# A two-layer decoder on one core: the second mixture of experts is computed on 31 sorted tiles instead of densely, and the variance guard moves into ScalarE's root

## The chip, the cores and the metric

The kernel runs on one core of one Trainium2 chip. The metric is the device time of one execution in microseconds; the figure for the kernel before is the median of 3 runs. Besides them there is one profiled execution with a trace, from which every row below is taken. Five engines work in parallel, each through its own instruction queue: TensorE (PE: matmuls and transposes), VectorE (DVE), ScalarE (ACT), GpSimd (POOL) and SyncE (SP), which here only issues DMAs.

## The reference, cut to what matters

The decoder has two layers over x of shape (4, 256, 256), that is 1024 tokens of 256 channels. Each layer is three residual sublayers with a layernorm ahead of each: layer 0 has an RWKV mixer, a cross attention with rotary keys and a mixture of 8 experts (one per token, with a capacity); layer 1 has grouped-query attention, a cross attention on latents and the mixture that is changed here:

```
16 experts, 2 per token, and 1 shared expert that is applied to every token
logits = h @ router_w.T;  weight = softmax over the two highest (bias is added for the choice only)
expert e: (silu(h @ Wu[e]) * (h @ Wg[e])) @ Wd[e]      Wu, Wg: 256 x 128,  Wd: 128 x 256
shared:   (silu(h @ Su) * (h @ Sg)) @ Sd               Su, Sg: 256 x 256,  Sd: 256 x 256
out = x + shared + w_first * expert_first + w_second * expert_second
```

The layernorm is (x - mean) / sqrt(var + 1e-5). In the grouped-query attention every query and key head of 128 numbers is normalised in the same way.

## The kernel before, in words

The program is written by hand per engine, in nine phases. At the end of each phase all of PE, DVE, ACT and POOL meet (the helper ended: each drains its engine, adds one to a semaphore and waits for the four). SP isn't part of that meeting; its loads wait for the phase numbers or for single results. Tiles of SBUF lie at fixed offsets, and a buffer of one phase is reused by the next. The eight PSUM banks are handed out in the order in which PE claims them (PsumBanks): each job has a key, PE waits until the bank's earlier job is emptied, and DVE or ACT wait until it is filled. The matmul of every product is issued in one helper (mm, L434) and every transpose in another (turn, L442); copies from PSUM are at L955 (ACT) and L1257 (DVE).

Layernorm (normalise) does four tiles of 128 tokens at a time: statistics on DVE (L1265, L1269), one tensor_scalar that adds 1e-5 to four variances (L1273), the root on ACT (L959), the reciprocal on DVE (L1275), and four passes that write the normalised tile (L1277). There are six such layernorms, of two groups each.

Phase 6 projects queries, keys and values of the grouped-query attention: for each of 8 token tiles six 512-column products on PE; five of them (40 units) go through squares on ACT (L1140), three products with the rotation tables on DVE (L1540 to L1542), a sum of squares per head (L1543), **the scaling by 1/128 and the addition of 1e-5 on DVE (L1546)**, the root on ACT (L1143), the reciprocal on DVE (L1554), an addition on POOL (L1773), four scalings on ACT (L1131), a second addition on POOL (L1779), and four transposes on PE, which follow their product by four units.

Phase 8 is the latent cross attention. While it runs, SP loads the mixture's weights.

Phase 9 is the mixture, dense: every expert is applied to all 1024 tokens, and the result is added with a weight that is zero for the experts that the token did not choose. The shared expert is treated as experts 17 and 18 with weight one. There are 36 units of (expert, half of the tokens). Products are taken in split form: each fp32 operand is a high part in the float32r type and a low part that holds the rest, and three single-pass products replace one fp32 product (split_product). ACT makes the high parts (L1208, L1214, L1220), POOL and DVE the low parts (L1823, L1831, L1605); ACT takes the silu (L1231), DVE the product (L1617) and the weighted additions into X (L1480). After the phase SP stores the 8 output tiles.

The first mixture (phase 5) is already routed: DVE computes a slot per token, POOL writes the rows by indirect DMA to HBM (L1759), SP reads them back in 5 groups (L1906), PE turns and multiplies them in plain fp32, SP writes the results of each expert (L1910), and POOL fetches each token's result by 8 indirect DMAs (L1766).

Of the kernel before, what the change touches and what calls it, by code (L numbers as in the profile page):

```python
# [38 lines left out]
E1X = E1 + 2  # L39
HKV = 4  # L40
# [39 lines left out]
def decoder(nc, x, ctx_512, L0_attn_Wk, L0_attn_Wv, L0_attn_Wr, L0_attn_Wo, L0_attn_time_decay, L0_attn_time_first,  # L80
# [5 lines left out]
    with ExitStack() as ctx:  # L86
# [15 lines left out]
        pool_tick = sb("pool_tick", [P, 8])  # L102
# [144 lines left out]

        m_wu = at("m_wu", 0, [P, E1X, KC, P])
        m_wg = at("m_wg", 65536, [P, E1X, KC, P])
        m_wd = at("m_wd", 83968, [P, E1X, C])  # L250
# [3 lines left out]
        m_su = at("m_su", 104416, [P, 2, HALF])  # L254
        m_h = at("m_h", 47104, [P, 3, HALF])

        m_hh = at("m_hh", 53248, [P, 3, HALF], F32R)
        m_hl = at("m_hl", 59392, [P, 3, HALF], F32R)
        m_wh = at("m_wh", 112672, [P, 3, 3, C], F32R)
        m_wl = at("m_wl", 121888, [P, 3, 3, C], F32R)  # L260
        m_HTh = at("m_HTh", 131104, [P, KC, B * T], F32R)
        m_HTl = at("m_HTl", 139296, [P, KC, B * T], F32R)
# [36 lines left out]
        x_high = sem("normalised_high_parts")  # L299
        x_low = sem("normalised_low_parts")  # L300
        w_high = sem("expert_weights_high_parts")
        w_low = sem("expert_weights_low_parts")
        h_high = sem("hidden_high_parts")
        h_low = sem("hidden_low_parts")
# [4 lines left out]
        hvar_ready = sem("head_variances_ready")  # L309
# [5 lines left out]
        ones_set = sem("ones_set")  # L315
        w_exp = sem("rwkv_exp_ready")
# [109 lines left out]
        def _(pe):  # L426
# [472 lines left out]
            pe.wait_ge(moe1_loaded, 16 * 11)  # L899
# [9 lines left out]
            def up1(key, by, i, n):  # L909

                e, cols = n // 2, slice(n % 2 * HALF, (n % 2 + 1) * HALF)
                if n % 2 == 0:
                    pe.wait_ge(w_low, 3 * (e + 1))
                if n < 2:
                    pe.wait_ge(x_low, 2 * (n + 1))
                ps = begin(key, by)
                k = lambda w, kc: w[:, e % 3, i, kc * P:(kc + 1) * P]
                split_product(ps, [(k(m_wh, kc), k(m_wl, kc), m_HTh[:, kc, cols], m_HTl[:, kc, cols])
                                   for kc in range(KC)]).then_inc(filled, 1)

            def down1(n):
                e, s = n // 2, n % 3
                pe.wait_ge(h_low, n + 1)
                for i in range(2):
                    ps = begin(("d1", n, i), "dve")
                    for tt in range(2):
                        o = (2 * i + tt) * P
                        last = split_product(ps[:, tt * C:(tt + 1) * C], [
                            (m_hh[:, s, o:o + P], m_hl[:, s, o:o + P], m_wh[:, e % 3, 2, :], m_wl[:, e % 3, 2, :])])
# [13 lines left out]
        def _(act):  # L943
# [29 lines left out]

            deviations(0, 0)
# [13 lines left out]
            def guarded(ct):  # L988
                act.wait_ge(decay_set, 1)
                act.wait_ge(scan_step, 2 * ct + 2)  # L990
                nc.scalar.activation(r_den[:, ct, :], r_den[:, ct, :], ACT.Identity, bias=pool_tick[:, 0:1]).then_inc(eps_added, 1)
# [142 lines left out]
            for n in range(5 * NT + 4):  # L1134
                if n < 5 * NT:
                    key = ("qkv", n // 5, n % 5)
                    act.wait_ge(*banks.filled(key))
                    if n >= 2:
                        act.wait_ge(hvar_ready, n - 1)
# [65 lines left out]
            for half in range(2):  # L1205
                for kc in range(KC):
                    cols = slice(half * HALF, (half + 1) * HALF)
                    nc.scalar.activation(m_HTh[:, kc, cols], HT[5][:, kc, cols], ACT.Copy).then_inc(x_high, 1)  # L1208

            def weights_high(e):  # L1210
                if e >= 3:
                    act.wait_ge(*banks.filled(("d1", 2 * e - 5, 1)))
                for i, w in enumerate((m_wu, m_wg, m_wd)):
                    nc.scalar.activation(m_wh[:, e % 3, i, :], expert(w, e), ACT.Copy).then_inc(w_high, 1)  # L1214

            def hidden_high(n):
                act.wait_ge(*banks.emptied(("g1", n)))
                if n >= 3:
                    act.wait_ge(*banks.filled(("d1", n - 3, 1)))
# [4 lines left out]
            for n in range(2 * E1X + 1):  # L1224
                if n < 2 * E1X:
# [3 lines left out]
                    if n >= 2:  # L1229
                        act.wait_ge(*banks.emptied(("g1", n - 2)))  # L1230
# [775 lines left out]
```

## Time and profile before

| | |
|---|---|
| median of 3 runs (lowest, highest) | 1479.85 us (1478.49, 1483.96) |
| the profiled execution's own time | 1472.4 us |
| its span | 1470.6 us |
| busy: PE, DVE, ACT, POOL | 1371.9, 878.8, 657.9, 861.6 us |
| granted TensorE clock, mean over the span | 0.959 |

A busy time is the sum of an engine's instruction spans within the span of the trace. TensorE's clock has two levels; the granted clock is given as a share of the higher one, 2.4 GHz. A plain fp32 product stands in the trace as two matmul records with two weight loads.

### The profile page before, as it was taken

To read this page: it belongs to the slowest core of one execution; us is meant where nothing else is said; L and a number is where in the kernel's file an instruction comes from. 1 tells how busy PE (TensorE), PEld (TensorE's weight loads), DVE (VectorE), ACT (ScalarE), POOL (GpSimd) and SP (SyncE) were. 2 spreads that over 40 slices of the span, in tenths; PEclk is the share of its full clock that TensorE was granted. 3 is DMA by queue.
4 is the path that set the end of the run, shared out by engine and by line. 5 is a ranking of instruction groups with operands and counts; after the bars stand their busy time and mean duration, and the time that the engine had idled before them with its cause. 6 is when DMAs were issued, how large, how long until landed. Compare 5 with 4: busy or idle time off the path is not lost.

```text
span 1470.6 us, 21064 instructions
## 1 busy us (share of the span) xinstructions
PE 1371.9 (93%) x7552; PEld 891.6 (61%) x7552; DVE 878.8 (60%) x1561; ACT 657.9 (45%) x1676; POOL 861.6 (59%) x789
## 2 busy tenths in 40 slices
PE   7999989999999999999989558998999989899998
PEld 4865545555555555555558434446777845578887
DVE  5756665666666666666513449995662147565555
ACT  4711123444444444444412217886661258733332
POOL 1284016889888888888841528885441036516554
PEclk9999988999999999999998769998999989989999
DMA  8401110000000000000036210000000042000000
GB/s 245 126 15 36 30 42 5 12 8 8 8 10 10 8 8 10 10 8 8 8 123 188 83 48 1 1 1 1 1 1 26 1 131 66 2 1 1 1 1 29
DMA packets 53374, 48.64 MB, mean 33 GB/s; under 512 B 18048, under 2 KB 49688, under 8 KB 52760
## 3 DMA queue, kind: packets, MB, share of 16 engines
q1 hardware_dynamic: 52504, 45.20, 11.2%
q0 software_dynamic: 768, 2.10, 0.4%
q8 instruction: 61, 1.00, 0.3%
q14 instruction: 41, 0.34, 0.1%
HBM read 34.18 MB, written 4.72 MB: 26 GB/s over the span
## 4 chain that ended last, share of the span: by engine, by line
PE 81%; ACT 6%; DVE 6%; issue 3%; POOL 3%; DMA 1%; POOLq 0%; DVEq 0%; SPq 0%; ACTq 0%
PE PS L434 76%; PE PS L442 4%; ACT s_sc L1173 2%; DVE s_mx L1567 1%; ACT a_m L1131 1%; POOL a_m L1779 1%; DVE HN L1277 1%; PE PS L588 1%; POOL a_m L1773 1%; ACT a_sq L1140 1%; ACT QKT L955 1%; DVE pm L1388 1%; POOL PWS L1720 0%; POOL slot_rows L1759 0%; PE PS L617 0%
## 5 line engine op out<-in xcount | busy, mean ns | idle before, releaser
L1720 POOL TENSOR_TENSOR PWS<-PWS 128x1024 f32<-128x1024 f32 x160 | 379.9, 2374 | 68.4 <-ACT PWS L1071 52.2
L1071 ACT ACTIVATE PWS<-PS 128x512 f32<-128x512 f32 (+1 forms) x416 | 227.9, 595 | 277.3 <-PE PS L434 264.9
L1388 DVE TENSOR_REDUCE pm<-PS 128x2 f32<-128x1024 f32 x192 | 227.4, 1220 | 77.0 <-PE PS L434 76.5
L434 PE MATMUL PS<-PWS,KVR 128*64 128x256 f32 (+1 forms) x1664 | 206.7, 386 | 0.0
L434 PE MATMUL PS<-QALL,KH 128*128 128x512 f32 (+1 forms) x416 | 187.2, 450 | 1.5 <-ACT PWS L1071 1.5
L434 PE MATMUL PS<-QM,KL 68*128 68x512 f32 (+1 forms) x416 | 165.9, 399 | 0.0
L434 PEld LDWEIGHTS PS<-PWS,KVR 128*64 128x64 f32 (+1 forms) x1664 | 109.5, 136 | 85.8 <-issue 34.5
L1794 POOL TENSOR_SCALAR s_sc<-s_sc,s_ri 128x128 f32<-128x128 f32 (+1 forms) x256 | 104.3, 429 | 94.6 <-DVE s_ri L1574 94.6
L434 PEld LDWEIGHTS PS<-QALL,KH 128*128 128x128 f32 (+1 forms) x416 | 77.6, 186 | 71.9 <-issue 35.9
L1173 ACT ACTIVATE s_sc<-PS,s_nb 128x128 f32<-128x128 f32 (+1 forms) x256 | 104.6, 432 | 4.5 <-DVE s_nb L1570 4.5
L1567 DVE TENSOR_REDUCE s_mx<-PS 128x2 f32<-128x512 f32 (+2 forms) x112 | 65.7, 611 | 50.0 <-PE PS L434 50.0
L434 PE MATMUL PS<-a_wT,HT 128*128 128x512 f32 x192 | 91.6, 610 | 0.7 <-ACTq L421 0.7
L434 PE MATMUL PS<-KH,QALL 64*128 64x512 f32 (+1 forms) x512 | 83.8, 414 | 6.2 <-DVE pm L1388 3.0
L1831 POOL TENSOR_TENSOR m_hl<-m_h,m_hh 128x512 fp32r<-128x512 f32 x36 | 46.9, 1302 | 64.4 <-ACT m_hh L1220 64.4
L434 PEld LDWEIGHTS PS<-QM,KL 68*128 68x128 f32 (+1 forms) x416 | 78.4, 188 | 8.2
L434 PE MATMUL PS<-z_HTh,z_w 128*128 128x512 f32 x192 | 68.7, 427 | 2.5 <-DVEq L421 2.5
L434 PEld LDWEIGHTS PS<-KH,QALL 64*128 64x128 f32 x512 | 39.5, 189 | 50.4 <-issue 34.8
L1411 DVE RECIPROCAL PS<-PS 128x256 f32<-128x256 f32 x32 | 56.2, 1757 | 21.4 <-PE PS L434 21.4
L1052 ACT ACTIVATE QALL<-PS 64x512 fp32r<-64x512 f32 x32 | 19.0, 594 | 111.6 <-PE PS L434 111.2
L1773 POOL TENSOR_TENSOR a_m<-a_m,a_m 128x512 f32<-128x512 f32 x40 | 50.8, 1270 | 29.5 <-DVE a_m L1542 29.5
L1231 ACT ACTIVATE m_su<-PS 128x512 f32<-128x512 f32 x36 | 21.5, 598 | 90.6 <-PE PS L434 90.5
L1617 DVE TENSOR_TENSOR m_h<-m_su,PS 128x512 f32<-128x512 f32 x36 | 24.7, 687 | 60.2 <-PE PS L434 60.2
(281 smaller groups left out, 2796.3 us busy)
## 6 DMA issues: line engine op xcount, KB each, us to landing
QALL<-qlo SPq DMA_DIRECT2D x32, 128.0 KB, 2.4
QM<-QALL SPq DMA_DIRECT2D x64, 64.0 KB, 2.0
f_w<-in_L_ffn_w_dram SPq DMA_DIRECT2D x2, 2048.0 KB
a_nat<-in_L_attn_w_qkv_dram SPq DMA_DIRECT2D x1, 3072.0 KB, 21.4
x_wq<-in_L_xattn_Wq_dram SPq DMA_DIRECT2D x1, 2048.0 KB, 11.0
x_wo<-in_L_xattn_Wo_dram SPq DMA_DIRECT2D x2, 1024.0 KB, 8.0
a_wo<-in_L_attn_w_o_dram SPq DMA_DIRECT2D x1, 2048.0 KB, 21.0
m_wd<-in_L_ffn_Wd_dram SPq DMA_DIRECT2D x1, 2048.0 KB, 8.4
```

The lines of the kernel that those rows point to most:

```text
L434: return nc.tensor.matmul(o, a, b, start=start, stop=stop, **kw)
L442: last = nc.tensor.transpose(ps[0:w, c:c + r], a, ident[0:r, 0:r])
L1071: nc.scalar.activation(PW[c][0:rows, j * HALF:(j + 1) * HALF], PS[0:rows, k % 2 * 512:(k % 2 + 1) * 512], ACT.Exp).then_inc(p_ready, 1)
L1173: ins = nc.scalar.activation(s_sc[:, k % 4, h, 0:nk], ps[:, j * nk:(j + 1) * nk], ACT.Exp, bias=s_nb[:, k % 3, h:h + 1], scale=scale, accu ...
L1388: ins = V.tensor_reduce(pm[u % 2][:, :, i // 3, i % 3], src, AX, ALU.max)
L1411: link(V.reciprocal(CTX_BANK[u % 2][:, 0:T], CTX_BANK[u % 2][:, 0:T]))
L1567: ins = V.tensor_reduce(s_mx[:, k % 3, i * per:(i + 1) * per], banks.bank(key)[:, 0:per * nk].rearrange("p (h k) -> p h k", h=per), AX, AL ...
L1617: V.tensor_tensor(m_h[:, n % 3, :], m_su[:, n % 2, :], ps, ALU.mult).then_inc(emptied["dve"], 1)
L1720: G.tensor_tensor(ACC[:, :], PW[0][:, :] if i == 0 else ACC[:, :], PW[i + 1][:, :], ALU.add).then_inc(acc_step, 1)
L1773: G.tensor_tensor(a_m1[:, n % 6, :], a_m1[:, n % 6, :], a_m2[:, n % 2, :], ALU.add).then_inc(m_sum, 1)
L1794: ins = G.tensor_scalar(s_sc[:, n % 4, h, 0:nk], s_sc[:, n % 4, h, 0:nk], s_ri[:, n % 4, h:h + 1], 1.0, ALU.mult, ALU.mult)
L1831: G.tensor_tensor(m_hl[:, n % 3, :], m_h[:, n % 3, :], m_hh[:, n % 3, :].bitcast(F32), ALU.subtract).then_inc(h_low, 1)
```

## The change

**Phase 9** is rewritten. Each of the 2048 (token, choice) pairs gets a slot in an array that is sorted by expert, with each expert's part padded to whole tiles of 128 rows; 2048 + 16 x 127 rows never need more than 31 tiles (TILES1), and all 31 are always computed. The slot comes from one-hots, two matmuls (the column counts and the rank within a tile) and a scan on DVE; the list of tokens per tile comes from 16 bf16 matmuls of one-hots (tile_tokens). SP stores the normalised rows of all tokens to HBM (xs1). POOL then fetches the 128 rows of each tile by an indirect DMA (31 of them, 8 buffers). For each tile PE turns the rows (2 transposes), multiplies by the expert's up and gate weights in one 256-column product over two parts of the channels, turns the hidden part (1 transpose) and multiplies by the down weights, all in plain fp32. The number of the expert of a tile is data: PE loads 31 registers from SBUF (value_load) before the loop, and the products take the weight's address from the register. DVE copies the turned rows and takes the gated product, ACT takes the silu and copies the hidden part and the result, SP stores the result tile to HBM (ys1). After all 31 tiles are stored, POOL fetches both results of each token by 16 indirect DMAs, DVE adds each with its weight, and SP stores each output tile as soon as it is final. The shared expert is computed densely: its up and gate products (shared_up) are placed among the routing steps, its down products (sd) after the tile loop.

Weights are loaded in another order and layout (up and gate side by side in m_wug; m_wd first, ten experts early, six later). The split products of phase 9 and all that fed them are gone.

**Layernorm and head norm**: the tensor_scalar that adds the guard is removed from both; ACT's root takes the variance directly, with 1e-5 as a bias from a small tile (guard) and, in phase 6, 1/128 as its scale. ACT now waits for the reduction itself (emptied) where it waited for the tensor_scalar.

```
 def deviations(k, g):
     act.wait_ge(var_ready, 2 * k + g + 1)
-    nc.scalar.activation(rstd[:, 4 * g:4 * g + 4], rstd[:, 4 * g:4 * g + 4], ACT.Sqrt).then_inc(std_ready, 1)
+    nc.scalar.activation(rstd[:, 4 * g:4 * g + 4], mv[:, 4 * g:4 * g + 4, 1], ACT.Sqrt,
+                         bias=guard[:, 0:1]).then_inc(std_ready, 1)
...
-    act.wait_ge(hvar_ready, n)
-    nc.scalar.activation(a_ss[:, (n - 1) % 4, :], a_ss[:, (n - 1) % 4, :], ACT.Sqrt).then_inc(hstd_ready, 1)
+    act.wait_ge(*banks.emptied(("qkv", (n - 1) // 5, (n - 1) % 5)))
+    nc.scalar.activation(a_ss[:, (n - 1) % 4, :], a_ss[:, (n - 1) % 4, :], ACT.Sqrt, bias=guard[:, 0:1],
+                         scale=1.0 / P).then_inc(hstd_ready, 1)
...
     V.tensor_reduce(a_ss[:, n % 4, :], a_sq[:, n % 2, :].rearrange("p (h d) -> p h d", h=4), AX,
                     ALU.add).then_inc(emptied["dve"], 1)
-    dve.wait_ge(*banks.emptied(key))
-    V.tensor_scalar(a_ss[:, n % 4, :], a_ss[:, n % 4, :], 1.0 / P, LN_EPS, ALU.mult, ALU.add).then_inc(hvar_ready, 1)
...
-r = rstd[:, 4 * g:4 * g + 4]
-V.tensor_scalar(r, mv[:, 4 * g:4 * g + 4, 1], LN_EPS, None, ALU.add).then_inc(var_ready, 1)
```

Phase 9 on PE, with the helpers that it calls:

```
+def shared_up(n):
+    half, it = divmod(n, 2)
+    for i, (name, by) in enumerate((("su", "act"), ("sg", "dve"))):
+        ps = begin((name, n), by)
+        for kc in range(KC):
+            last = mm(ps, m_wug[:, E1 + it, kc, i * P:(i + 1) * P], HT[5][:, kc, half * HALF:(half + 1) * HALF], kc == 0, kc == KC - 1)
+        last.then_inc(filled, 1)
+def tile_up(j):
+    pe.wait_ge(*banks.emptied(("ex", j)))
+    ps = begin(("eu", j), "dve")
+    for kc in range(KC):
+        last = mm(ps[:, 0:2 * P], e_xT[:, j % 2, kc, :], m_wug[:, bass.ds(of_tile[j], 1), kc, :], kc == 0, kc == KC - 1)
+    last.then_inc(filled, 1)
...
 logits1()
-for n in range(2 * E1X + 2):
-    if n < 2 * E1X:
-        up1(("u1", n), "act", 0, n)
-        up1(("g1", n), "dve", 1, n)
-    if n >= 2:
-        down1(n - 2)
+shared_up(0)
+rank1()
+for n in range(1, 4):
+    shared_up(n)
+tile_tokens()
+pe.wait_ge(eid_ready, 1)
+of_tile = [pe.value_load(e_eid[0:1, j:j + 1], min_val=0, max_val=E1 - 1) for j in range(TILES1)]
+for j in range(-1, TILES1 + 2):
+    if j + 1 < TILES1:
+        rows_turned(j + 1)
+    if 0 <= j < TILES1:
+        tile_up(j)
+    if 0 <= j - 1 < TILES1:
+        hidden_turned(j - 1)
+    if 0 <= j - 2:
+        tile_down(j - 2)
+pe.wait_ge(*banks.emptied(("sg", 3)))
+for t in range(NT):
+    out_product(("sd", t), [(e_hs[:, it, t * P:(t + 1) * P], m_wd[:, E1 + it, :]) for it in range(2)])
```

Phase 9 on POOL and the end of SP's queue:

```
+pool.wait_ge(xs1_stored, 32)
+pool.wait_ge(ids_ready, 1)
+for j in range(TILES1):
+    if j >= 8:
+        pool.wait_ge(*banks.filled(("ex", j - 8)))
+    G.indirect_dma_start(e_x[:, j % 8, :], None, xs1, IndirectOffsetOnAxis(ap=e_ids[:, j:j + 1], axis=0), ...).then_inc(tile_back[j % 8], 16)
+for i in range(4):
+    pool.wait_ge(tile_sent[i], 16 * len(range(i, TILES1, 4)))
+for t in range(NT):
+    for k in range(2):
+        G.indirect_dma_start(e_yg[:, t, k, :], None, ys1, IndirectOffsetOnAxis(ap=e_idx[:, k * NT + t:k * NT + t + 1], axis=0), ...).then_inc(both_back[t], 16)
...
-sp.wait_ge(phase_ended, 4 * 9)
+for j in range(TILES1):
+    sp.wait_ge(*banks.emptied(("ey", j)))
+    sp.dma_start(ys1[j * P:(j + 1) * P, :], e_y[:, j % 4, :]).then_inc(tile_sent[j % 4], 16)
 for t in range(NT):
+    sp.wait_ge(x_final, t + 1)
     sp.dma_start(ov[t], X[:, t, :]).then_inc(stored, 16)
```

PE's queue behind the logits read as follows before (m_HTh, m_HTl: high and low parts of the tokens; m_wh, m_wl: of the weights):

```order
L434 MATMUL PS<-m_rT,HT 128x16 x16
L434 MATMUL PS<-m_HTh,m_wh 128x512
L434 MATMUL PS<-m_HTl,m_wh 128x512
L434 MATMUL PS<-m_HTh,m_wl 128x512
L434 MATMUL PS<-m_HTh,m_wh 128x512
```

and these three forms, later mixed with those of the down products, fill the queue to the end. Now, from the shared expert's last products to the third tile (e_x, e_xT: rows of a tile as fetched and turned; e_h, e_hT: hidden part; e_eid: experts of the tiles; ISA rows are register instructions; a fp32 product is one row here):

```order
L472 MATMUL PS<-HT,m_wug 128x512 x12
L472 MATMUL PS<-e_A,e_B 128x64 x16
L1005 TENSOR_LOAD e_eid
L1005 ISA x2
...
L480 MATMUL PS<-ident,e_x 128x128 x2
L472 ISA
L472 MATMUL PS<-m_wug,e_xT 128x256
L472 ISA
L472 MATMUL PS<-m_wug,e_xT 128x256
L480 MATMUL PS<-ident,e_h 128x128
L472 ISA
L472 MATMUL PS<-m_wd,e_hT 128x256
```

The pair TENSOR_LOAD and ISA x2 stands there 31 times in a row, between the bf16 products of tile_tokens and the first tile; each of the three expert products of a tile has one register instruction ahead of it.

In phase 6 DVE's queue read as follows for one unit before (a_m: rotated parts; a_ss: sums of squares):

```order
L1540 TENSOR_TENSOR a_m_154<-PS,a_gc 128x512
L1541 TENSOR_TENSOR a_m_155<-PS,a_gs 128x4x64
L1542 TENSOR_TENSOR a_m_155<-PS,a_gs 128x4x64
L1543 TENSOR_REDUCE a_ss<-a_sq 128x4
L1546 TENSOR_SCALAR a_ss<-a_ss 128x4
L1554 RECIPROCAL a_ss<-a_ss 128x4
```

and now, where L1546 has gone and nothing came in its place (the line numbers of the changed kernel):

```order
L1619 TENSOR_TENSOR a_m_154<-PS,a_gc 128x512
L1620 TENSOR_TENSOR a_m_155<-PS,a_gs 128x4x64
L1621 TENSOR_TENSOR a_m_155<-PS,a_gs 128x4x64
L1622 TENSOR_REDUCE a_ss<-a_sq 128x4
L1631 RECIPROCAL a_ss<-a_ss 128x4
```

The reciprocal, which belongs to the unit before, now follows the reduction directly.

## Rows read from the trace of the kernel before

**Rows 1.** The page: busy time, share of the span, instructions

```profile
PE 1371.9 (93%) x7552; PEld 891.6 (61%) x7552; DVE 878.8 (60%) x1561; ACT 657.9 (45%) x1676; POOL 861.6 (59%) x789
```

**Rows 2.** Busy time by stretch: phase 6, phase 9, the output stores

```profile
core 0: us, PE busy (x) PEld busy (x) DVE busy (x) ACT busy (x) POOL busy (x), PEclk, DMA share, GB/s
876.00:1000.00 124.00, 110.11 (x352) 52.22 (x352) 108.61 (x242) 97.69 (x288) 100.10 (x80) 0.95 0.00 1
1304.40:1465.00 160.60, 158.99 (x898) 139.88 (x898) 93.48 (x205) 63.50 (x136) 84.24 (x90) 0.97 0.00 1
1465.00:1470.60 5.60, 0.00 (x0) 0.00 (x0) 0.00 (x0) 0.00 (x0) 0.00 (x0) 0.85 0.56 187
```

**Rows 3.** Chain that ended last, phase 9: start us, us, what

```profile
1305.24 24.89 PE PS L434 x114
```

**Rows 4.** Phase 6: one token tile, a wait, a group, instructions, pieces of the chain

```profile
919.00:933.20 14.20, 13.15 (x46) 6.27 (x45) 13.42 (x30) 12.16 (x37) 12.49 (x11) 1.00 0.00 0
PE PS L442 <- POOL a_m L1779: 12.0, 24, 2.3
L1546 DVE TENSOR_SCALAR a_ss<-a_ss 128x4 f32<-128x4 f32 x40 | 30.0, 750 | 1.4
930.00 1.26 POOL L1773 TENSOR_TENSOR a_m<-a_m,a_m 128x512 f32<-128x512 f32 x1 [0.19 <-DVE a_m L1542]
930.54 0.75 DVE L1546 TENSOR_SCALAR a_ss<-a_ss 128x4 f32<-128x4 f32 x1
875.89 3.79 PE PS L434 x4
890.58 3.45 PE PS L434 x8
```

**Rows 5.** The last layernorm: its guard on DVE

```profile
1299.72 0.17 DVE L1273 TENSOR_SCALAR rstd<-mv 128x4 f32<-128x4 f32 x1
```

**Rows 6.** DVE at the start of phase 9: from the logits to the first choice

```profile
1312.36 0.29 DVE L1257 COPY f_l<-PS 128x128 f32<-128x128 f32 x1 [4.05 <-PE PS L434]
1314.83 0.29 DVE L1444 TENSOR_TENSOR f_oh<-f_v,f_mx 128x128 f32<-128x128 f32 x1
```

**Rows 7.** Granted clock around PE's stops, stretches of 5 us

```profile
825.00:830.00 5.00, 3.07 (x13) 2.83 (x14) 0.69 (x1) 1.88 (x2) 3.38 (x10) 0.50 0.86 263
830.00:835.00 5.00, 5.00 (x32) 4.46 (x32) 0.69 (x1) 1.48 (x3) 4.09 (x11) 0.94 0.00 0
1310.00:1315.00 5.00, 5.00 (x18) 4.42 (x19) 2.40 (x9) 0.00 (x0) 0.26 (x1) 0.50 0.00 0
```

**Rows 8.** The first mixture: transposes, products, indirect DMAs, a result's way back

```profile
807.26 3.79 PE L442 MATMUL PS<-ident,a_wo 128*128 128x128 f32 x32
811.19 1.62 POOL L1759 DMA_INDIRECT slot_rows<-HN,f_idx  x1 [0.31 <-issue]
850.12 3.62 PE L434 MATMUL PS<-f_w,f_hT 128*80 128x256 f32 x16
853.77 0.69 DVE L1515 COPY f_y<-PS 80x512 f32<-80x512 f32 x1 [1.04 <-PE PS L434]
857.32 1.07 POOL L1766 DMA_INDIRECT f_yg<-slot_results,f_idx  x1 [21.00 <-DMA slot_results<-f_y]
858.70 1.01 POOL L1766 DMA_INDIRECT f_yg<-slot_results,f_idx  x1 [0.30 <-issue]
DMA to landing us min/median/max: 2.7/2.8/2.9
```

**Rows 9.** Work of a queue: a register move, an issue, a DMA to landing

```profile
L1766 POOLq MOVE  x8: 29/29/29, 856.5 to 860.2; - x8
L1910 SPq DMA_DIRECT2D slot_results<-f_y x8: 304/305/336, 834.6 to 854.5; - x8
out_dram<-X SPq DMA_DIRECT2D x8, 128.0 KB, 1.8
```

More of the change, by code:

```diff
@@ new lines, in rank1, with tile_tokens @@
+            def rank1():
+                pe.wait_ge(choice_ready, 1)
+                ps = begin("rank1", "dve")
+                both = e_any[:, :, :].rearrange("p e t -> p (e t)")
+                mm(ps[:, 0:P], e_trim, both)
+                mm(ps[:, P:2 * P], ones[:, :], both).then_inc(filled, 1)
+            def tile_tokens():
+                ps = begin("ids", "dve")
+                for n in range(2 * NT):
+                    if n % NT == 0:
+                        pe.wait_ge(onehot_ready, n // NT + 1)
+                    last = mm(ps[:, 0:64], e_B[:, n, :], e_A[:, n, :, :].rearrange("p s j -> p (s j)"), n == 0, n == 2 * NT - 1)
+                last.then_inc(filled, 1)
@@ new lines, in rows_turned @@
+            def rows_turned(j):
+                pe.wait_ge(tile_back[j % 8], 16 * (j // 8 + 1))
+                turn(("ex", j), "dve", [e_x[:, j % 8, kc * P:(kc + 1) * P] for kc in range(KC)])
+            def tile_up(j):
+                pe.wait_ge(*banks.emptied(("ex", j)))
+                ps = begin(("eu", j), "dve")
+                for kc in range(KC):
+                    last = mm(ps[:, 0:2 * P], e_xT[:, j % 2, kc, :], m_wug[:, bass.ds(of_tile[j], 1), kc, :],
+                              kc == 0, kc == KC - 1)
+                last.then_inc(filled, 1)
@@ L990, in guarded @@
                 act.wait_ge(scan_step, 2 * ct + 2)
-                nc.scalar.activation(r_den[:, ct, :], r_den[:, ct, :], ACT.Identity, bias=pool_tick[:, 0:1]).then_inc(eps_added, 1)
+                nc.scalar.activation(r_den[:, ct, :], r_den[:, ct, :], ACT.Identity, bias=guard[:, 1:2]).then_inc(eps_added, 1)
             for ct in range(KC):
@@ L1204, in _ @@
             copy_out("mrT", m_rT[:, :, :], lambda ps: ps[:, 0:KC * E1])
[L1205 to L1214, printed above, removed]
@@ new lines, in _, with gate @@
+            nc.scalar.activation(f_e[:, :, :], f_e[:, :, :], ACT.Exp).then_inc(e_exp, 1)
+            for n in range(4):
+                ps = banks.take(("su", n), "act")
+                act.wait_ge(*banks.filled(("su", n)))
+                nc.scalar.activation(e_su[:, n, :], ps, ACT.Silu).then_inc(emptied["act"], 1)
+            def gate(j):
+                act.wait_ge(*banks.filled(("eu", j)))
+                if j >= 2:
+                    act.wait_ge(*banks.emptied(("eu", j - 2)))
+                nc.scalar.activation(e_st[:, j % 2, :], banks.bank(("eu", j))[:, 0:P], ACT.Silu).then_inc(tile_silu, 1)
@@ new lines, in hidden_out, with result_out @@
+            def hidden_out(j):
+                if j >= 2:
+                    act.wait_ge(*banks.filled(("ey", j - 2)))
+                copy_out(("eh", j), e_hT[:, j % 2, :], lambda ps: ps[:, 0:P])
+            def result_out(j):
+                if j >= 4:
+                    act.wait_ge(tile_sent[j % 4], 16 * (j // 4))
+                copy_out(("ey", j), e_y[:, j % 4, :], lambda ps: ps[:, 0:C])
+            for j in range(TILES1 + 2):
+                if j < TILES1:
+                    gate(j)
+                if 0 <= j - 1 < TILES1:
+                    hidden_out(j - 1)
+                if 0 <= j - 2:
+                    result_out(j - 2)
@@ new lines, in _ @@
+            link(V.tensor_reduce(e_ef[:, :], e_past[:, :, :], AX, ALU.add))
+            link(V.tensor_scalar(e_ef[:, :], e_ef[:, :], float(E1 - 1), None, ALU.min))
+            V.tensor_copy(e_eid[:, :], e_ef[:, :]).then_inc(eid_ready, 1)
+            for n in range(1, 4):
+                hidden(n)
+            ps = banks.take("ids", "dve")
+            dve.wait_ge(*banks.filled("ids"))
+            V.tensor_reduce(e_idf[:, :], ps[:, 0:64].rearrange("p (s j) -> p j s", s=2), AX, ALU.add).then_inc(emptied["dve"], 1)
```

285 lines of the change are left out of this document (168 added, 117 removed).

## Prediction

> **What bounds the kernel now.** Start with the page: PE is busy for 93% of the span, no other engine for more than 60% [rows 1]. Then the stretches. Phase 9 takes 160.6 us, and PE is busy for 159.0 of them at a clock of 0.97, with no DMA [rows 2]. The chain agrees: from 1305.24 on it stays in PE's products [rows 3]. What shortens PE's work there shortens the kernel, until something else is last. Phase 6 is different: in one token tile of 14.20 us PE is busy for 13.15, DVE for 13.42, POOL for 12.49, ACT for 12.16 [rows 4]. Three engines are nearly full, and PE waits 12.0 us in all for POOL's second addition, whose input is late because DVE is. Behind phase 9 lie 5.6 us of stores [rows 2].
>
> **Phase 6: minus 6.5.** L1546 works on 4 columns and takes 0.750 us, 40 times [rows 4]. Its twin in the layernorm, L1273, takes 0.17 [rows 5]. The example shows why: it starts at 930.54 and ends at 931.29, while POOL's addition runs from 930.00 to 931.26; it ends when POOL ends [rows 4]. So its removal gives DVE back about 0.66 us per unit, not 0.17. With it away DVE needs 13.42 - 5 x 0.66 = 10.1 us per token tile, and PE's 13.15 is the highest load. If PE had no wait left, 8 x (14.20 - 13.15) = 8.4 us would go. POOL (12.49) and ACT (12.16) stay close below, with uneven work, so I take 6.5; the bounds are 0 and 8.4. The Trainium skill, SBUF — State Buffer, section "Who interferes with whom", says that a DVE tensor_scalar in a two-port mode and a GpSimd instruction exclude each other for a whole instruction. The trace agrees (0.750 beside 0.17), and by the instruction's own size alone the gain on DVE would have been 40 x 0.17 = 7 us instead of 26, which at 0.17 per unit leaves DVE the most loaded engine.
>
> **Layernorms: minus 0.9.** L1273 goes from each of twelve groups: 0.17 us and an issue gap of 0.03 [rows 5]. It lies on the path only where PE waits for normalised tiles, which is the second group of a layernorm behind a phase, and the first group at the start. Of the twelve I count five, a choice: 1.0, of which I take 0.9. The guard on ACT's bias costs nothing: the small tile is set by POOL some 5 us before the first variance.
>
> **Phase 9, from its start at 1304.4.** Turning the router's weights and the logits stay as they are: DVE gets the logits at 1312.36 [rows 6].
>
> Routing on DVE: eight steps from there to 1314.83 are 0.31 us each [rows 6]. Seven more to the sum of both choices give 1317.3. PE has meanwhile done the first quarter of the shared products: a record of 512 columns takes (3.79 - 1.22)/3 = 0.86 us at the low clock, where 1.22 is the first record with its latency (so 0.86 is an estimate from the piece), and 3.45/8 = 0.43 at the high one [rows 4]. The clock is still at 0.50 until 1315 [rows 7], so three records are slow and the other 29 fast: 2.6 + 12.5 = 15.1 us. The two rank products and the sixteen bf16 ones are about 2.1 more, and the wait for DVE at 1317 is 0.4. PE is through at 1312.2 + 17.6 = 1329.9. DVE's rank and one-hot steps (some fourteen of 0.2 to 0.3, and 512 to 1024 columns wide ones, together about 8 us) end at 1326 and lie beside the shared products; the list of experts follows by 1328. So do the moved loads: they run in phase 8, as before, and are over long before its end.
>
> The registers: 31 loads with two register instructions each stand alone on PE. No row shows a load. A register move on a queue takes 0.029 us [rows 9], so 3 x 0.029 x 31 = 2.7 us is the lower bound. A full DMA round to landing, 1.8 us [rows 9], bounds it above: 31 x 1.86 = 57.7. A load is a request by a sequencer that waits for an answer from memory, nearer to the issue of a DMA (0.30 us [rows 9]) than to a transfer. I take half as much again, 0.45, + 0.06 for its two moves, 15.8 us, until 1345.7. The first rows of tokens have landed by then (ids two short DVE steps after PE's 1329.9, at 1330.5, and 2.8 to landing [rows 8], so 1333.3); nothing else hides the loads.
> The Trainium skill, DMA: Bandwidth & Descriptors, section "Latency and other measured facts", gives a floor of about 600 ns for such a load. By it the term would be 31 x 0.66 = 20.5 us, 4.7 more than by my value. No row here shows it.
>
> The tile loop: three transposes at 3.79/32 = 0.12 and six records of 256 columns at 3.62/16 = 0.226, both taken at the high clock [rows 8], are 0.36 + 1.36 = 1.72 us. Three register moves add 0.09 [rows 9]: 1.81. A copy of 128 columns takes 0.29 [rows 6]; with three instructions of 128 to 256 columns on ACT and two on DVE I estimate 1.1 and 0.75 per tile, beside PE's work on other tiles, so PE sets the period. POOL needs 1.01 + 0.30 = 1.31 per indirect DMA [rows 8], with 8 buffers ahead. 31 x 1.81 = 56.1. PE has stood still for 16 us before, so the loop begins at the low clock; after a stop of like length it was back within 3 to 8 us of work (0.50, then 0.94 [rows 7]), which costs half of that, I take 3. The last tile needs 2.2 more for silu, product, transpose, down product and copy. End: 1345.7 + 61.3 = 1407.0.
>
> The way back: 857.32 - (853.77 + 0.69) = 2.9 us from a result's copy to POOL's first fetch [rows 8]; then 15 x 1.31 = 19.7 to the last of sixteen fetches, 2.8 to its landing, 0.5 for the last addition, 0.4 to issue the store (0.30 and the wait) and 1.8 to land [rows 9]. That is 28.1: the end is 1435.1. The shared down products, their additions, and seven of the eight stores lie beside the fetches. Before, the end was 1470.6: minus 35.5.
>
> **The sum.** -35.5 - 6.5 - 0.9 = -42.9. The profiled execution took 1472.4 us around its span of 1470.6 and would take 1429.5. The median of the runs is 7.5 higher, at 1479.85; the same difference gives 1437.
>
> **Rivals.**
> - *The register loads are nearly free* (0.09 instead of 0.51 each). For it: no row shows a load, and a move takes 29 ns. Against it: an answer from memory has to come before the register instruction behind it. Then PE waits for the first rows instead, until about 1333.5: -12, 1425. Chance 0.13.
> - *The loads cost a transfer each*, 1.0 to 1.86: at 1.86 it is +41.9, 1479, no change; at 1.2, +23, 1460. Chance 0.14. Equal to before it would be at (42.9 + 15.8)/31 = 1.89 per load, just above the bound.
> - *Slower than before:* the product whose address comes from a register isn't prepared behind the running one. Each of three then shows its latency, about 0.4 us, and PE, idle for a third of the time, stays at the low clock, where its work is 3.4 us. The period is 3.4 + 0.1 + 1.2 = 4.7, +89.6 - 3, 1524. For it: PE at 0.50 while it was idle [rows 7]. Against it: the first mixture's products ran at 0.94 and above within 5 us. It decides from a period of 1.81 + 45.9/31 = 3.3 us. At the low clock alone it would be 3.5, 1486, hardly slower. Chance 0.07 for both.
> - *Rows come late.* Where DVE works on two SBUF tiles, an indirect DMA took 1.62 + 0.31 instead of 1.31 [rows 8]. At 1.93 per tile POOL sets the period: +3.7, 1441. It stays within the forecast, as does a phase 6 that gives nothing (1443).
>
> **From this to the numbers.** The forecast with its variants holds 0.66, from 1427 to 1448. The range of 8 in 10 takes in the free loads and loads up to about 1.3: 1417 to 1464. A measurement of this kernel tells 0.5%, or 7 us, from no change. Faster by more than that are the forecast, free loads and most of the dear loads: 0.90. Within it: loads near the upper bound and a loop at about 3.2 us, 0.05. Slower: 0.05.
>
> **What would show it.** In phase 6, PE's wait for POOL's second addition below 4 us and a token tile at about 13.4. In phase 9, a gap on PE of about 16 us between the bf16 products and the first transpose of e_x; a period of 1.8 us with PE busy for over 90% and the clock back at 1.00 within four tiles; sixteen fetches 1.31 apart; 28 us from the last tile to the end. The prediction is wrong if the gap is over 30 us or under 4, if the period is above 2.2 (then ask whether PE's clock, its queue or POOL's fetches set it), or if fetches of padded rows are slower than those of the first mixture.

## The result, and the profile after

The changed kernel takes 1432.76 us (median of four runs, 1431.55 to 1438.27), beside 1479.17 for the kernel before on the same chip (four runs, 1477.78 to 1483.96). The ratio is 0.9693, with a 95% interval from 0.9668 to 0.9718. The profiled execution took 1432.66 us around its span of 1430.9. Forecast were 1437 and a span of 1427.7.

The page of the profile after, first part, answers to [rows 1]:

```profile
PE 1298.3 (91%) x7051; PEld 815.5 (57%) x7051; DVE 808.5 (57%) x1439; ACT 627.3 (44%) x1642; POOL 822.6 (57%) x747
```

PE has 73.6 us less work, but the span is shorter by 39.7 only: the rest is time in which PE now stands still. The busy times by stretch show where (columns as in [rows 2]): phase 6, one token tile of it, phase 8, phase 9 up to the tile loop, the loop, its steady part, and the way back to the end.

```profile
876.00:1000.00 124.00, 112.66 (x367) 55.06 (x368) 83.92 (x204) 99.60 (x289) 102.56 (x81) 0.95 0.00 1
925.21:939.28 14.07, 13.14 (x46) 6.26 (x45) 10.16 (x26) 12.29 (x37) 12.38 (x11) 1.00 0.00 0
1180.70:1303.60 122.90, 112.10 (x875) 64.27 (x875) 70.24 (x212) 78.42 (x301) 55.79 (x133) 0.92 0.26 70
1303.60:1347.60 44.00, 24.40 (x84) 14.86 (x84) 17.80 (x49) 5.26 (x7) 8.08 (x8) 0.69 0.09 25
1347.68:1402.23 54.55, 54.15 (x281) 44.76 (x282) 21.89 (x62) 25.47 (x92) 22.93 (x23) 0.95 0.53 126
1354.00:1394.00 40.00, 40.00 (x222) 33.73 (x221) 17.37 (x50) 20.24 (x74) 19.94 (x20) 1.00 0.64 146
1402.00:1430.90 28.90, 7.04 (x33) 5.87 (x31) 11.05 (x24) 0.38 (x1) 15.95 (x16) 0.66 0.39 120
```

In the loop PE is full, and in its steady part at the high clock (1.00; 0.95 over the whole loop); before it PE stands still for 19.6 of 44.0 us, and behind it for 21.9 of 28.9. Those two stretches are where the gain stopped. In phase 6 DVE has 24.7 us less to do than in [rows 2], but the token tile went only from 14.20 ([rows 4]) to 14.07.

The gap ahead of the loop, in the chain that ended last (start us, us, what), and what PE's sequencer does in it, in the view of the line with the loads (count, ns min/median/max, first and last start):

```profile
1330.15 3.29 DMA e_x<-token_rows,e_ids
1333.44 14.25 issue
1347.68 0.67 PE PS L480 x2
```

```profile
L1005 PEldq TENSOR_LOAD <-e_eid x31: 294/301/492, 1327.2 to 1346.9; - x31
L1005 PEldq FUSED_REGOPS  x31: 146/146/165, 1327.7 to 1347.3; - x31
L1005 PEldq SEQ_ASSERT  x31: 18/18/24, 1328.0 to 1347.5; - x31
```

The first rows were there at 1333.44. From then on the chain shows "issue": nothing outside PE is waited for. It is PE's own sequencer, which goes through 31 loads from 1327.2 to 1347.6, 0.657 us each, 20.4 us in all. The tile loop, in the same chain:

```profile
1353.70 0.87 PE PS L472 x4
1354.56 0.11 PE PS L480
1354.67 0.43 PE PS L472 x2
1355.11 0.22 PE PS L480 x2
1355.32 0.87 PE PS L472 x4
```

One tile is 0.87 + 0.11 + 0.43 + 0.22 = 1.63 us of records without a gap. And the end, where the last pieces are POOL's last fetches and their landing:

```profile
1422.17 1.00 POOL e_yg L1958
1423.17 0.30 issue
1423.47 1.00 POOL e_yg L1958
1424.47 0.30 issue
1424.78 2.86 DMA e_yg<-tile_results,e_idx
1427.69 0.04 issue
1427.73 0.50 DVE X L1766
1428.25 0.48 DVE X L1768
```

### The profile page after: what moved, and what is told of

The parts are those of the page before. It is cut to its first block, busy times and chain, and to the rows that moved or that the text cites. A ratio compares the mean times of both kernels' runs of the same rounds, so it can differ in the third digit from the quotient of the medians.

```text
span 1430.9 us, 20175 instructions
## 1 busy us (share of the span) xinstructions
PE 1298.3 (91%) x7051; PEld 815.5 (57%) x7051; DVE 808.5 (57%) x1439; ACT 627.3 (44%) x1642; POOL 822.6 (57%) x747
## 4 chain that ended last, share of the span: by engine, by line
PE 78%; POOL 5%; DVE 5%; ACT 5%; issue 4%; DMA 1%; POOLq 0%; SPq 0%; DVEq 0%; ACTq 0%
PE PS L472 72%; PE PS L480 5%; ACT s_sc L1255 2%; POOL a_m L1908 2%; POOL a_m L1902 1%; DVE s_mx L1644 1%; ACT a_m L1212 1%; DVE HN L1356 1%; POOL e_yg L1958 1%; DVE pm L1467 1%; POOL PWS L1849 0%; POOL slot_rows L1888 0%; PE PS L655 0%; PE PS L626 0%; POOL s_sc L1923 0%
## 5 line engine op out<-in xcount | busy, mean ns | idle before, releaser
L1952 POOL DMA_INDIRECT e_x<-token_rows,e_ids x31 | 31.0, 1001 | 74.4 <-DVE e_ids L1734 49.2
L1377 DVE TENSOR_TENSOR X<-X,PS 128x256 f32<-128x256 f32 x40 | 16.8, 419 | 84.5 <-PE PS L472 84.5
L1243 ACT ACTIVATE s_pt<-PS 128x512 f32<-128x512 f32 x64 | 38.4, 602 | 50.1 <-PE PS L480 50.1
```

Source lines behind the costliest of these rows:

```text
L1243: nc.scalar.activation(s_pt[:, m % 2, 0, :], ps, ACT.Copy).then_inc(emptied["act_turned"], 1)
L1952: G.indirect_dma_start(e_x[:, j % 8, :], None, xs1, IndirectOffsetOnAxis(ap=e_ids[:, j:j + 1], axis=0), bounds_check=B * T - 1, oob_is_err ...
```

## Experiments

Nine further kernels ran, and three kernels a second time, in three groups, each with runs of the kernel before on the same chip beside them (medians 1472.28, 1477.96 and 1471.12). Since those differ, ratios are compared, or lengths of phases read from the traces. The lengths are these (us; the first row is the kernel before). "phase 6" is from its first product to the start of its last transpose, "phase 8" from its first product to phase 9's first product. "p9 to loop" is from phase 9's first product to the first transpose of fetched rows, "loop to last copy" from there to the start of the last result's copy:

| kernel | median | ratio [95%] | phase 6 | phase 8 | p9 to loop | loop to last copy |
|---|---|---|---|---|---|---|
| before | 1479.17 | 1 | 123.3 | 120.2 | | |
| changed | 1432.76 | 0.9693 [0.9668, 0.9718] | 118.8 | 122.9 | 44.1 | 54.6 |
| roots alone | 1471.74 | 0.9988 [0.9964, 1.0011] | 118.8 | 123.0 | | |
| mixture alone | 1436.24 | 0.9749 [0.9684, 0.9813] | 123.3 | 127.1 | 43.4 | 53.8 |
| root ahead | 1431.36 | 0.9698 [0.9656, 0.9739] | 118.8 | 122.9 | 44.1 | 54.5 |
| loads inside | 1425.95 | 0.9671 [0.9627, 0.9714] | 118.8 | 122.9 | 29.9 | 62.5 |
| loads inside, root ahead | 1420.58 | 0.9625 [0.9560, 0.9691] | 120.2 | 127.1 | 29.5 | 54.2 |
| 15 loads inside | 1423.46 | 0.9641 [0.9589, 0.9694] | 118.8 | 122.9 | 34.3 | 54.4 |
| no register | 1420.23 | 0.9617 [0.9567, 0.9667] | 118.7 | 122.9 | 30.0 | 54.7 |
| eight fetches | 1424.36 | 0.9634 [0.9579, 0.9688] | 120.2 | 127.0 | 43.8 | 53.6 |
| short bias | 1423.61 | 0.9691 [0.9635, 0.9746] | 112.6 | 122.0 | 44.2 | 54.6 |

These lengths repeat: in the three kernels that were traced twice they differ by less than 0.1 us. What lies ahead of phase 6 doesn't repeat. Phase 6 starts at 875.9 and 873.4 us in the two traces of the kernel before, and at 876.0 and 879.1 in those of the changed one.

**The two halves of the change apart.** First the kernel before with the new roots alone:

```
-    V.tensor_scalar(a_ss[:, n % 4, :], a_ss[:, n % 4, :], 1.0 / P, LN_EPS, ALU.mult, ALU.add).then_inc(hvar_ready, 1)
...
-    nc.scalar.activation(a_ss[:, (n - 1) % 4, :], a_ss[:, (n - 1) % 4, :], ACT.Sqrt).then_inc(hstd_ready, 1)
+    nc.scalar.activation(a_ss[:, (n - 1) % 4, :], a_ss[:, (n - 1) % 4, :], ACT.Sqrt, bias=guard[:, 0:1],
+                         scale=1.0 / P).then_inc(hstd_ready, 1)
```

> The dense mixture stays, and only the two guards move into the root. From the traces of before and after: phase 6 ends 4.4 us earlier, the start of the kernel is 2.7 us later (the table load for the first root now stands behind the wait for the variances, 1.28 us, and the transposes after it run longer at the low clock), of which 0.5 is left when phase 3 starts. Theory one (the first root's table load is exposed, phase 6 gives 4.4): about 4 us faster than before, 1475, with the first normalised tile 1.4 us later. Rival (the record's sum: 6.5 from phase 6 and 0.9 from the layernorms, the late start is chance): 7.4 us faster, 1472, and no late start in this trace.

And the changed kernel with the old roots (the same lines the other way):

> The tiled mixture with the old guards on DVE. If the parts add up, this is the kernel after plus 4 us: about 1437, and the first table load is back ahead of the first wait, at 0.7 us in the trace. If the moved loads of phase 8, and not chance in the clock, cost the 2.7 us by which phase 8 is longer after than before (122.1 us beside 119.5), phase 8 is about 122 us here too and about 119.5 in the kernel with the guards alone; if it is the clock's chance, the two don't differ in this way.

The roots alone give 0.9988, which is no change that the runs can tell: the interval goes from 5.3 us faster to 1.6 slower, so it still holds the first theory's 4 us and rules out the rival's 7.4. Yet phase 6 is 4.5 us shorter, as in the changed kernel. In the trace of this execution phase 8 takes 2.8 of them back, phase 9 0.7, and phase 6 starts 1.4 later than in the kernel before. The mixture alone gives 0.9749, 36.0 us of 1472.28; its trace has phase 6 at its old length and phase 8 at 127.1. So most of the gain is phase 9's, and the 0.56% between this ratio and the changed kernel's, whose intervals overlap, is what phases 6 and 8 differ by in the traces.

**A root ahead of the first wait.** ACT's queue at the start: before, the root's table was loaded at 0.74, while ACT had nothing to do. In the changed kernel two waits stand ahead of the root, for the guard and for the variances. The wait for the variances is an instruction of its own there, at 6.98, and the load comes behind it. The timeline of ACT in the kernel before and in the changed one:

```profile
0.74 1.28 ACT L959 ACT_TABLE_LOAD   x1 [0.74 <-PEq L1992]
7.00 0.21 ACT L959 ACTIVATE rstd<-rstd 128x4 f32<-128x4 f32 x1 [4.97 <-DVE rstd L1273]
```

```profile
7.03 1.28 ACT L1038 ACT_TABLE_LOAD   x1 [7.03 <-DVE mv L1350]
8.33 0.30 ACT L1038 ACTIVATE rstd<-mv,guard 128x4 f32<-128x4 f32 x1
```

The next kernel is the changed one with a small root between the two waits:

```
 act.wait_ge(guard_set, 1)
+nc.scalar.activation(guard[:, 2:3], guard[:, 0:1], ACT.Sqrt)
 deviations(0, 0)
```

> The kernel after, with one more root on ScalarE, of one column that nobody reads, ahead of the first layernorm's. Theory: the table load moves into the wait for the inputs; the first normalised tiles come 1.3 us earlier and phase 2 starts up to 2.7 us earlier; of that 0.5 to 1 us reaches the end, since most of the late start has been made up by phase 3 (1432). Rival: a later start is simply passed through, and the end comes 2.7 us earlier (1430).

```profile
0.74 1.28 ACT L1055 ACT_TABLE_LOAD   x1 [0.74 <-PEq L2140]
2.04 0.20 ACT L1055 ACTIVATE guard<-guard 128x1 f32<-128x1 f32 x1
7.73 0.30 ACT L1038 ACTIVATE rstd<-mv,guard 128x4 f32<-128x4 f32 x1 [5.49 <-DVE mv L1351]
```

The load is ahead again and 1.28 us are off the first root's path; but the inputs landed 0.7 us later in that execution, and the ratio, 0.9698, doesn't differ from the changed kernel's. The price of the table load is shown by the lines, its worth in the whole time is below what the runs tell.

**Loads inside the loop.** The register of tile j + 1 is loaded behind tile j's up products (expert_loaded(j) is the value_load of tile j):

```
-of_tile = [pe.value_load(e_eid[0:1, j:j + 1], min_val=0, max_val=E1 - 1) for j in range(TILES1)]
+expert_loaded(0)
...
     if 0 <= j < TILES1:
         tile_up(j)
+    if 0 <= j < TILES1 - 1:
+        expert_loaded(j + 1)
```

> The kernel after, with each tile's expert loaded into its register inside the tile loop, behind the tile's up products, instead of all 31 ahead of it. Theory one (the loads hold only PE's queue, and the products already issued cover them): the loop starts when the first rows have landed, 1333.4 instead of 1347.7, and keeps about 1.63 us per tile: 14 us faster than after, 1419. Rival (a load stops the queue for 0.66 us and nothing covers it): 2.29 us per tile, so 20.4 us are added to the loop and 19.8 taken away ahead of it: no change, 1433. In between, with a part covered, for instance 1.9 us per tile: 1427.

The loop begins 29.9 us behind phase 9's start instead of 44.1, and its steady period is 1.63 as before: a load inside costs nothing. The whole gained less than that: the ratio, 0.9671, has an interval that overlaps with the changed kernel's. The last copy came only 6.3 us earlier against phase 9's start, since this execution had one stop, in its chain:

```profile
1341.14 0.02 ACT e_y L1042
1341.16 5.68 another core or an unknown queue
1346.84 0.28 ACT e_st L1307
```

ACT starts at 1346.84, while the products that it takes ended at 1344.34 by PE's records, 2.5 us earlier; DVE had come 1.4 us late to the transposes before. PE, which waits for both, stands still and is back at the low clock (0.50) from 1345 on. Two readings were left: that the early start of the loop brings this about, or that it was that execution's own. The same edit ran again, together with the root ahead:

> The changed kernel with both earlier edits together: a small root ahead of the first wait, and the load of tile j+1's register inside the loop behind tile j's up products. Theory A (the stall of some 5 us at 1341 in the run with loads inside the loop belongs to the early start of the loop: ScalarE and VectorE have not stood still before it): the stall is seen again a few us behind the loop's start, and the time is some 8 us below the changed kernel, 1425 plus or minus 3. Theory B (the stall was a mishap of that one execution, and its median was low by chance): no stall, loop start 1331.5 and period 1.63, the way back begins 16 us earlier, time 1418. The root ahead adds nothing in either.

There is no such stop: from the first transpose at 1337.90 to the last copy at 1392.09 PE is busy for 53.7 of 54.2 us.

```profile
1337.90:1392.09 54.19, 53.70 (x281) 44.26 (x282) 21.90 (x62) 25.43 (x93) 28.27 (x29) 0.96 0.62 143
```

Against phase 9's start the last copy comes 15.0 us earlier than in the changed kernel, and the median is 1420.58, at 0.9625 the lowest ratio of any version that computes the reference. An early start of the loop alone doesn't bring the stop about; the kernels below start it early too and have none. But none of these is the kernel in which it was seen. That one was traced once, and its three other runs took 1424.00, 1427.36 and 1430.50 us, at most 0.5 less than the traced one with its stop (1424.53). So it isn't shown that the stop was that execution's own, and what it was the trace doesn't say.

**Sixteen loads ahead, fifteen inside.**

```
+for j in range(16):
+    expert_loaded(j)
...
+    if 15 <= j < TILES1 - 1:
+        expert_loaded(j + 1)
```

> The changed kernel with 16 of the 31 register loads ahead of the loop (16 x 0.657 = 10.5 us) and the other 15 inside it, each behind the up products of the tile before. Theory A (each load ahead of the loop costs 0.657 us on the way to the end, each one inside nothing): loop start 9.9 us earlier, at 1337.8 on the changed kernel's clock, period 1.63 in both halves, span 9.9 shorter, 1423 in time. Theory B (the loop's end cannot be earlier than about 8 us before the changed kernel's, because something else, such as the stall seen when all loads were inside, holds it): loop start at 1337.8 but a stall behind it, span 6 to 8 shorter, 1425 to 1427, the same as with all loads inside.

Loop start 34.3 us behind phase 9's, 9.8 less than 44.1; 15 x 0.657 is 9.9. The 16 loads ahead still set it, since the rows have landed 4.4 us before:

```profile
1330.84 3.30 DMA e_x<-token_rows,e_ids
1334.14 4.40 issue
1338.54 0.67 PE PS L480 x2
```

So each load ahead of the loop costs its 0.657 us until the first rows' landing takes its place, and each one inside nothing: the first theory, in size too. The span is 8.9 us shorter for 9.9 expected; phase 6 starts 0.7 later in this trace, and the way back takes 0.4 more.

**No register.** Tile j takes expert j mod E1, which is 16 (the text of what was expected says 8, wrongly), at a fixed address, in the up products and, in the same way, in the down products:

```
-of_tile = [pe.value_load(e_eid[0:1, j:j + 1], min_val=0, max_val=E1 - 1) for j in range(TILES1)]
+of_tile = [j % E1 for j in range(TILES1)]
...
-        last = mm(ps[:, 0:2 * P], e_xT[:, j % 2, kc, :], m_wug[:, bass.ds(of_tile[j], 1), kc, :],
+        last = mm(ps[:, 0:2 * P], e_xT[:, j % 2, kc, :], m_wug[:, of_tile[j]:of_tile[j] + 1, kc, :],
```

> The changed kernel with no register at all: tile j is multiplied by the weights of expert j mod 8 at a fixed address, so the second mixture's values are not the reference's; all else stays, the wait for the expert list too. Theory A (a register-addressed product costs nothing beyond its loads): the loop starts 20.4 us earlier, its period stays 1.63, and the time is that of the kernel with loads inside the loop less at most 0.7 (one load): some 1425, stall included. Theory B (reading the address from a register costs PE some of the 1.63): the period falls below 1.55 and the loop of 31 tiles is over 2.5 us shorter. Theory C (the loads' own work inside the loop made the stall): without loads there is no stall and the time is 1412 to 1415.

Its chain in the steady loop:

```profile
1354.32 0.87 PE PS L472 x4
1355.18 0.11 PE PS L480
1355.29 0.43 PE PS L472 x2
1355.73 0.22 PE PS L480 x2
1355.95 0.87 PE PS L472 x4
```

1.63 again, to the hundredth. The address from a register costs PE nothing that can be seen. The loop starts at 30.0, as with the loads inside, where the landing of the first rows sets it. The time, 1420.23, is that of the version with loads inside and the root ahead, 1420.58. That there was no stop says nothing for the third theory, since that version has its loads inside the loop and had none either.

**Eight fetches.**

```
-for k in range(2):
+for k in range(1):
     G.indirect_dma_start(e_yg[:, t, k, :], ...)
...
-dve.wait_ge(both_back[t], 32)
+dve.wait_ge(both_back[t], 16)
...
-V.scalar_tensor_tensor(X[:, t, :], e_yg[:, t, 1, :], e_w[:, 1, t:t + 1], ...)
+V.scalar_tensor_tensor(X[:, t, :], e_yg[:, t, 0, :], e_w[:, 1, t:t + 1], ...)
```

> The changed kernel with 8 final fetches instead of 16: the rows of each token's second choice are not fetched, and the first choice's rows are used with the second weight, so the output is not the reference's. Theory A (the end is a queue of fetches on GpSimd, 1.30 us each, and nothing else behind it): way back 28.3 - 8 x 1.30 = 17.9 us from the last result's copy to the end, time 10.4 lower, 1422. Theory B (the fetches share the DMA queues, and the last one's landing of 2.86 us or VectorE's additions set the end): less than 6 us lower, 1427 or more. Theory C (VectorE, with two weighted additions for each tile, is the bound of this stretch): no change.

From the last copy at 1407.05 to the end at 1425.8 it is 18.75 us, where it was 1430.9 - 1402.23 = 28.7: 9.9 less, for 8 x 1.30 = 10.4 expected. POOL's busy time in the stretch is that of eight fetches:

```profile
1407.05:1425.80 18.75, 6.81 (x32) 5.66 (x30) 10.77 (x24) 0.38 (x1) 8.35 (x8) 0.81 0.41 126
```

The end is a queue of fetches on POOL. The whole is lower by 5.1 us of span only, since phases 6 and 8 took 120.2 and 127.0 us here.

**What holds phase 6.** POOL's second addition is done for one of four heads:

```
-G.tensor_tensor(m1, m1, a_bt[:, i, s, :].unsqueeze(1).to_broadcast([P, 4, P]), ALU.add)
+G.tensor_tensor(m1[:, 0:1, :], m1[:, 0:1, :], a_bt[:, i, s, :].unsqueeze(1).to_broadcast([P, 1, P]), ALU.add)
```

> The changed kernel with GpSimd's addition of the bias table in phase 6 done for the first of four heads only (128 of 512 elements), so the token mixture's scores and the output are not the reference's. Theory A (GpSimd, busy 12.6 of 14.07 us in each token tile, is what now holds phase 6, since the products and the transposes wait for its additions): the tile's period falls by 0.5 us or more, to 13.5 or less, and phase 6 by 4 us or more from 118.8. Theory B (PE's own chain of products, transposes and copies sets the 14.07 and GpSimd only keeps up with it): the period stays at 14.0 to 14.1, and phase 6 loses less than 2 us, at its end. Phase 8's low stretch can add or hide 3 to 7 us of the whole time, so the phase's length is what is read.

One token tile of it, and PE's wait in phase 6 (us in total, times, longest), first of this kernel, then of the changed one:

```profile
923.73:936.83 13.10, 12.87 (x45) 6.35 (x44) 10.16 (x26) 12.18 (x37) 8.42 (x10) 1.00 0.00 1
```

```profile
PE PS L480 <- POOL a_m L1908: 5.6, 11, 1.6
```

```profile
PE PS L480 <- POOL a_m L1908: 9.9, 18, 1.8
```

The tile's period is 13.10 instead of 14.07, DVE's work in it is the same 10.16, PE's nearly so (12.87 and 13.14), and POOL's is 4.0 less. The phase is 6.2 us shorter. So with DVE relieved it was POOL's addition that held the tile at 14.07, be it by POOL's load or by the time of each addition on the way to its transposes; the run doesn't separate the two. The ratio, 0.9691, doesn't show the 6.2 us (the changed kernel's is 0.9693); the spans of the two traces do, 1423.8 and 1430.9.

**Phase 8 once more.** Its length differed between kernels that are alike up to its end. The kernel before, the one with the new roots alone and the changed one were each looked at again, in one execution:

> The kernel before, once more, to see how long the second stretch at the low clock in phase 8 is. It was 7 us in the profile of before (phase 8 120.2 us from its first product to phase 9's), 13 to 14 us in five profiles of kernels with the new roots and in one with them alone (122.9), and 24 us in three others, one of which has the old roots (127.1). Theory A (the length comes from one execution to the next, among a few values, in every kernel): a second look at the kernel before gives 120.2, 122.9 or 127.1, any of them. Theory B (it hangs on when the kernel reaches phase 8 or on what ScalarE did before, so on the new roots): 120.2 again.

> The kernel before with the new roots alone, once more. Theory A (the length of the low stretch in phase 8 is drawn anew in each execution): phase 8 takes 120.2, 122.9 or 127.1. Theory B (it goes with the new roots): 122.9 again. Phase 6, from first product to last transpose, is 118.8 in either.

> The changed kernel, once more. Theory A (drawn anew in each execution): phase 8 takes 120.2, 122.9 or 127.1. Theory B (a property of the kernel): 122.9 again. All else as before it: 20.4 us of register loads, loop period 1.63, way back 28.3 to 28.7.

Phase 8 took 120.2, 122.9 and 123.0 us: each kernel as the first time. Times of one run: 1469.99, 1472.31 and 1435.86. The difference is a stretch at the low clock. At 1208 us the kernel before has PE at 1.00, the changed one at 0.50, with PE equally busy:

```profile
1208.00:1210.00 2.00, 2.00 (x22) 1.31 (x20) 1.46 (x7) 1.71 (x8) 1.41 (x4) 1.00 0.00 0
```

```profile
1208.00:1210.00 2.00, 2.00 (x16) 1.12 (x14) 1.05 (x5) 1.57 (x8) 1.53 (x4) 0.50 0.00 0
```

In both the clock falls between 1196 and 1199, when PE, full until then, has been busy for 1.16 of 2 us. It is low for 7 us in both traces of the kernel before, for 13 to 14 in six kernels and in both repeats with the new roots, for 10 with the short bias, and for 24 in three kernels: the mixture with the old roots, the loads inside with the root ahead, and the eight fetches. The theory that the length is drawn anew in each execution has three repeats against it. The theory that it goes with the new roots fails too: the mixture with the old roots is among the longest. The moved weight loads don't decide it, since the roots alone, with the old loads, show 123.0. What does is open; it wasn't tried to move the phase's start alone.

## Why the prediction was right

The forecast's case came: routing, loads in a row, a loop bound by PE, a queue of fetches. The span fell by 39.7 us instead of 42.9, made up of misses of both signs.

- **Start of phase 9: -7.4 forecast, -1.7 measured.** The terms "phase 6: minus 6.5" and "layernorms: minus 0.9" were mis-sized.
  - *Phase 6* gave 4.5 (3.1 in two of the later kernels). DVE's relief was right: its load in a tile went from 13.42 to 10.16 us (10.1 forecast). But "POOL (12.49) and ACT (12.16) stay close below" was priced at 1.9 us, and POOL was the limit: the six steady tiles fell by 0.14 us each, and the rest of the 4.5 came in the first tile (2.0) and at the end (1.6). The wait for POOL's second addition was put down to DVE's lateness, but with DVE relieved most of it stayed. The signs that were named, a wait for POOL below 4 us and a tile of 13.4, did not come (9.9 us, where it is 13.5 in the same window before, and 14.07). The wait came near, and the tile went below, only when POOL's addition was cut (5.6 us, 13.10). The Trainium skill's rule in "SBUF — State Buffer", section "Who interferes with whom", is that a DVE instruction in a two-port mode and a GpSimd instruction keep each other out for a whole instruction. The trace agrees with it: DVE's busy time fell by 24.7 us, where the instruction by its own size would give 7.
  - *Layernorms*: "The guard on ACT's bias costs nothing" was wrong at the start. The new wait put the 1.28 us table load behind the variance, and the root with a bias tile takes 0.30 us instead of 0.21, in every layernorm: about half of the 0.20 that goes with L1273 is taken back. Phase 6 starts at 876.0 and [rows 4]'s 875.89, so nothing of the 0.9 is seen, but in the second traces it starts at 879.1 and 873.4, so that pair can't tell 0.9 us either way.
  - *Phase 8*, 2.7 us longer, had no term.
  - In the second traces phase 9 starts 3.9 us later than before, and the spans differ by 34.1 (1434.0 and 1468.1). So the -1.7 rests on one pair of traces, while the -4.5 and the +2.7 came both times.
- **Routing and shared products**: PE was through 23.6 us after phase 9's first product, where 24.7 was forecast (1312.2 + 17.6 is 1329.8, not 1329.9, which changes nothing). Right.
- **The registers: 15.8 forecast, 20.4 measured**, within 2.7 to 57.7. The Trainium skill's floor, "DMA: Bandwidth & Descriptors", section "Latency and other measured facts", gave 20.5 with the register moves added, and was nearer than the row of a DMA's issue that I went by; the floor itself, about 600 ns, is near the 0.657 from one load to the next and not the load's own 0.301. The mis-sized term is the 0.45 + 0.06 per load. The load itself took 0.301 us, as much as that issue, and less than my 0.45; the two steps behind it took 0.146 and 0.018 for my 0.06, and the gaps between all of them, 0.19, had no term. The register moves of 0.029 were no measure of it.
- **The tile loop: 61.3 forecast from its start to the last copy's end, 54.9 measured.** The steady period is 1.63, not 1.81: the three register instructions, 0.09, hide behind the products, and a record of 256 columns takes 0.217, not 0.226. What stands beside 31 x 1.63 = 50.5, the start at the low clock and the last tile, is 4.4 us, for 5.2 forecast.
- **The way back: 28.1 forecast, 28.3 measured**, with fetches 1.30 apart.

In phase 9 the misses are 3.7 (the loads and the earlier end of the products), -6.4 and 0.2; with the 5.7 ahead of it that is 3.2, the difference of 39.7 to 42.9. That the sum came so near is in part luck: a loop 6.4 us too dear paid for most of what phases 6 and 8 and the loads cost more. The median, 4.2 below the forecast's 1437, missed on the other side: the runs' median stands 0.1 us above the profiled run's time here, and the 7.5 that it stood above it in the runs of before were added to the forecast.

Of the rivals, nearly free loads and loads that cost a transfer are both ruled out by 0.657 us. The slower case, the register-addressed product that is not prepared behind the running one, is ruled out by the chain without gaps, and by the kernel without registers. Rows did not come late: the fetches took 0.994 to 1.102 us each.

The best version is the change with its register loads inside the loop and the root ahead of the first wait: 1420.58 us, ratio 0.9625, 10 us below the changed kernel by the ratios, though the two intervals just overlap. In the traces the span is 10.2 lower: 15.0 us less from phase 9's first product to the last copy, of which phases 8 and 6 took back 4.2 and 1.4 in this trace.

## What to carry to other kernels

Put loads of addresses into registers where the engine's queue is full of work, one tile ahead, and not in a row ahead of the loop: a load of 0.66 us is free behind 1.6 us of products. When an engine's load drops, ask first which other engine stood next below it: here POOL, at 12.5 of 14.2, took the place of DVE at 13.4. A row of indirect fetches at the end costs its queue time of 1.3 us each, so what bounds the end is their number.

## What the runs showed that was not expected

- A product whose weights' address comes from a register ran exactly as fast as one with a fixed address: a tile of 1.63 us in both.
- Loading a register from SBUF took 0.301 us for the load, 0.146 for the register operations and 0.018 for the bounds check, 0.657 from one to the next, and nothing when products ran beside it.
- The stretch at the low clock in phase 8 lasted 7, 10, 13 to 14, or 24 us, the same for the same kernel in all three repeats, and differed between kernels with the same code up to its end. It moves the whole by up to 7 us, as much as the new roots were to bring. The two kernels with a phase 6 of 120.2 us are among those with the longest.
- One execution had ACT start 2.5 us and DVE 1.4 us after their inputs were ready, between 1341 and 1347 us; with the low clock behind it this made the loop 8 us longer. Nine other traces of this loop, none of them of the same kernel, show nothing of the kind, and its cause stays open.
